# Order of the first transfers in a delta-rule attention and mixture-of-experts kernel, and matmuls of constants at its beginning

## What is computed

```python
q = (x @ Wq).reshape(b, n, H, DK)          # H = 4, DK = 128
k = (x @ Wk).reshape(b, n, H, DK)
v = (x @ Wv).reshape(b, n, H, DV)          # DV = 32
beta = jax.nn.sigmoid(x @ Wb)
k = k * jax.lax.rsqrt(jnp.sum(k * k, axis=-1, keepdims=True) + 1e-12)
def step(S, inp):                          # scanned over the 2048 positions
    q_t, k_t, v_t, b_t = inp
    pred = jnp.einsum('bhk,bhkv->bhv', k_t, S)
    delta = (v_t - pred) * b_t[..., None]
    S = S + k_t[..., :, None] * delta[..., None, :]
    return (S, jnp.einsum('bhk,bhkv->bhv', q_t, S))
```

## Time and profile before

| | us |
|---|---|
| median of 3 runs (lowest, highest) | 524.82 (523.22, 527.61) |
| the profiled execution's own time | 524.84 |
| its span | 523.1 |
| attention phase (TensorE's first expert matmul starts at) | 319.9 |
| one chunk in the steady part, from `t128_copy` of one chunk to the next (51.13 to 68.78) | 17.65 |

### The profile page before, as it was taken

The page is one execution under the profiler, slowest core; times in us unless marked ns, Lnnn a source line. Parts: engine busy times, 40 slices in busy tenths (PEclk is TensorE's granted clock), DMA queues, the critical chain, the costliest instruction groups (busy, mean ns, idle before and its releaser), DMA issues.

```text
span 523.1 us, 19041 instructions
## 1 busy us (share of the span) xinstructions
PE 467.4 (89%) x7181; PEld 389.0 (74%) x7181; DVE 314.9 (60%) x1209; ACT 327.8 (63%) x905; POOL 292.2 (56%) x445
## 2 busy tenths in 40 slices
PE   6979999999999999999898988999999999999900
PEld 4656766777667776776665677999999999999900
DVE  4435467667686676766875764644555545555345
ACT  3545668877888778878675634555555555555463
POOL 3055517638377383682753341567777767767652
PEclk9998999999999999999997999999999999999965
DMA  3367763552335514336161113354655545553376
GB/s 96 32 113 186 217 172 58 111 90 33 71 50 85 84 26 77 51 54 99 31 174 42 34 47 93 47 112 55 119 107 77 111 56 123 95 82 32 31 151 201
DMA packets 148084, 46.10 MB, mean 88 GB/s; under 512 B 107168, under 2 KB 141600, under 8 KB 148000
## 3 DMA queue, kind: packets, MB, share of 16 engines
q1 hardware_dynamic: 132848, 29.86, 29.0%
q0 software_dynamic: 13568, 9.51, 13.1%
q10 hardware_dynamic: 1584, 5.59, 2.8%
HBM read 21.39 MB, written 23.55 MB: 86 GB/s over the span
## 4 chain that ended last, share of the span: by engine, by line
PE 69%; issue 9%; ACT 9%; DMA 7%; DVE 2%; SPq 2%; POOL 1%; ACTq 0%; DVEq 0%; POOLq 0%
PE ps L1004 17%; PE ps L1015 11%; PE ps L730 5%; PE ps L681 4%; ACT TT L1126 3%; PE ps L684 2%; PE ps L761 2%; PE ps L737 2%; PE ps L812 2%; PE ps L881 2%; PE ps L896 2%; PE ps L800 2%; PE ps L1030 2%; PE ps L870 2%; PE ps L842 2%
## 5 line engine op out<-in xcount | busy, mean ns | idle before, releaser
L1784 POOL DMA_INDIRECT x_store<-xk,row x80 | 125.7, 1571 | 65.0 <-ACT xk L1275 45.5
L1603 DVE TENSOR_TENSOR hb<-ps,hs 128x320 f32<-128x320 f32 (+1 forms) x128 | 62.5, 491 | 44.6 <-ACT hs L1267 44.0
L1744 POOL DMA_INDIRECT slots_in<-x,slot x64 | 63.5, 992 | 25.4 <-issue 16.6
L1267 ACT ACTIVATE hs<-ps 128x320 f32<-128x320 f32 (+1 forms) x128 | 55.2, 435 | 32.0 <-PE ps L1004 31.2
L1004 PE MATMUL ps<-xeTh,w13h 128*128 128x320 f32 x224 | 70.5, 315 | 1.0 <-DVE xeTl L1627 1.0
L1004 PE MATMUL ps<-xeTh,w13l 128*128 128x320 f32 x224 | 69.2, 309 | 0.0
L1004 PE MATMUL ps<-xeTl,w13h 128*128 128x320 f32 x224 | 69.1, 309 | 0.0
L1015 PE MATMUL ps<-w2s,hb 128*128 128x128 f32 x512 | 64.3, 278 | 0.1
L1015 PEld LDWEIGHTS ps<-w2s,hb 128*128 128x128 f32 x512 | 59.8, 192 | 2.2 <-DVE hb L1603 0.3
L1757 POOL TENSOR_TENSOR Vk<-V,sq 128x256 f32<-128x256 f32 x16 | 10.4, 647 | 86.7 <-ACT sq L1109 86.6
L1275 ACT ACTIVATE xk<-ps,gs 128x128 f32<-128x128 f32 x80 | 24.2, 364 | 44.9 <-PE ps L1030 35.3
(11 more groups left out here) (218 smaller groups left out, 1147.5 us busy)
## 6 DMA issues: line engine op xcount, KB each, us to landing
slots_in<-zeros ACTq DMA_DIRECT2D x10, 520.0 KB, 4.2
xe<-slots_in SPq DMA_DIRECT2D x15, 325.0 KB, 2.9
w<-w_in SPq DMA_DIRECT2D x8, 448.0 KB, 4.3
xTs<-xT SPq DMA_DIRECT2D x4, 512.0 KB, 5.5
a_diag<-hb SPq DMA_DIRECT2D x64, 32.0 KB
inv<-xs SPq DMA_DIRECT2D x16, 128.0 KB
xi<-inv SPq DMA_DIRECT2D x16, 128.0 KB
xk<-x SPq DMA_DIRECT2D x8, 256.0 KB, 3.6
```

What stands on the lines that cost most here:

```text
L1267: af(hs[to, s % 4, :], ps[src, HB[fill_of(s) % 5], 0:HALF], ACT.Silu).then_inc(hs_ready, 1)
L1603: v.tensor_tensor(hb[to, par, c, HALF * g:HALF * g + HALF], ps[rows_, at, 0:HALF], hs[rows_, s % 4, :], ALU.mult).then_inc(h_ready, 1)
L1744: g.indirect_dma_start(out=xs_d[:, :], out_offset=bass.IndirectOffsetOnAxis(ap=to, axis=0), in_=x1[:, p % 2, j, k, :], in_offset=None,).th ...
L1784: g.indirect_dma_start(out=x1_d[:, :], in_=ye[:, par, i, :], in_offset=None, out_offset=bass.IndirectOffsetOnAxis(ap=row[:, par, i:i + 1], ...
```

## The change

Five edits, with the loop of SP, ACT's `clear` and the start of TensorE touched:

1. The first inverse is stored one step earlier in SP's program (step 2, after chunk 1's `load_blocks`, before chunk 2's `send_blocks`), and loaded in step 3 before chunk 2's `load_blocks` instead of behind them.
2. The second x^T chunk is issued in step 1, behind chunk 1's `send_blocks`, instead of in step 3.
3. The zeros are issued at a fixed table of places: three in ACT's steps 4 and 5, eight from (6, 2) to (7, 5).
4. `avg` is the first thing DVE sets, with a semaphore of its own, and TensorE multiplies it by itself 5 times before anything else (`begin_on(5)`).
5. `keep_on(22)` in step 4 becomes `keep_on(10)`.

```diff
--- before.py
+++ after.py
@@ -51,6 +51,8 @@
 LAST = 9
 
 YR, AR, VR = 4, 4, 4
+
+CLEARS = ((4, 3), (4, 5), (5, 1), (6, 2), (6, 3), (6, 4), (6, 5), (7, 0), (7, 2), (7, 4), (7, 5))
 
 
 def order_of_fills():
@@ -342,6 +344,7 @@
         xs_zero = sem("xs_zero")
         consts_pool = sem("consts_pool")
         consts_dve = sem("consts_dve")
+        avg_made = sem("avg_made")
         setup_mm = sem("setup_mm")
         setup_act = sem("setup_act")
         setup_dve = sem("setup_dve")
@@ -572,19 +575,24 @@
 
             for p in range(NP + LAST):
                 if p == 3:
+                    load_inverse(0)
+                at(load_blocks, p - 1)
+                if p == 2:
                     send_inverse(0)
-                at(load_blocks, p - 1)
                 if p == 4:
                     send_inverse(1)
                 if p > 4:
                     at_group(send_inverse, p - 2)
-                at(load_inverse, p - 3)
+                if p > 3:
+                    at(load_inverse, p - 3)
                 at(store_x1, p - 6)
-                if p in (3, 5, 8):
-                    load_xT(1 + (3, 5, 8).index(p))
+                if p in (5, 8):
+                    load_xT(2 + (5, 8).index(p))
                 if p in (4, 7, 11, 15):
                     load_xk((4, 7, 11, 15).index(p))
                 at(send_blocks, p)
+                if p == 1:
+                    load_xT(1)
                 if p == NP + 1:
                     load_weights(0, 0)
                     load_weights(1, 1)
@@ -918,6 +926,13 @@
                 for _ in range(n):
                     mm(ps[:, CB, 0:P], ident[:], ident[:], start=True, stop=True)
 
+            def begin_on(n):
+
+                pe.wait_ge(avg_made, 1)
+                for _ in range(n):
+                    mm(ps[:, CB, 0:P], avg[:], avg[:], start=True, stop=True)
+
+            begin_on(5)
             setup_keys()
             pe.wait_ge(wv_ld, 16)
             pe.wait_ge(setup_act, 1)
@@ -942,7 +957,7 @@
                 if p == NP + 5:
                     keep_on(36)
                 if p == 4:
-                    keep_on(22)
+                    keep_on(10)
                 at(z_32, p - 4)
                 at(outputs, p - 5)
                 at(project_x, p - 5)
@@ -1182,11 +1197,13 @@
 
             def clear(p, i):
 
-                k = 6 * (p - 6) + i - 2
-                if 0 <= k < XS_ZEROS:
+                if (p, i) not in CLEARS:
+                    return
+                k = CLEARS.index((p, i))
+                if k < XS_ZEROS:
                     act.dma_start(xs_d[k * 8 * P:(k + 1) * 8 * P, :].rearrange("(p r) d -> p (r d)", p=P),
                                   zeros[:]).then_inc(xs_zero, 16)
-                if k == XS_ZEROS:
+                else:
                     act.dma_start(xs_d[ROWS:ROWS + SPARE, :].rearrange("(p r) d -> p (r d)", p=P),
                                   zeros[:, 0:SPARE // P * W]).then_inc(xs_zero, 16)
 
@@ -1322,12 +1339,12 @@
             link = Link(dve, link_dve)
             v = nc.vector
 
+            v.memset(avg[:], 1.0 / P).then_inc(avg_made, 1)
             for t in (TT, xi, Zs, x64):
                 v.memset(t[:], 0.0)
             v.memset(eps[:], EPS)
             v.memset(tiny[:], 1e-12)
             v.memset(one[:], 1.0)
-            v.memset(avg[:], 1.0 / P)
             dve.wait_ge(consts_pool, 5)
 
             link(v.tensor_scalar(pbit[:], pidx[:], 16, None, ALU.bitwise_and))
```

## The result

| | median of the runs, us | profiled execution, us | its span, us |
|---|---|---|---|
| before, on the same chip | 525.07 (4 runs) | | |
| changed | 532.47 (531.79 to 534.68, 4 runs) | 534.68 | 532.9 |

The ratio is 1.0139, with a 95% interval of 1.0102 to 1.0177: slower by 1.4%, 7.4 us. The forecast was 523.0 us in a range that ended at 526.2. The profiled execution is the slowest of the four, so its differences from before (10 us by the span) are a little larger than those of the medians.

A forecast was written before the change was run, and what follows sets the result against it. TensorE, busy 89% of 523.1 us, was taken as the bound, with early waits on SP's queue and landings targeted. Only 1.8 us was to pass DVE's gate: 524.84 - 1.8 = 523.0 us, range 519.8 to 526.2.

The forecast's parts named there:

- keep_on(10) at nothing: Step 4 wait on TensorE: shorter fill, 2.3 instead of 5.07 us, costs at most the present low clock, so nothing.
- The beginning: TensorE's start: earlier matmuls raise the clock sooner, 1.3 us gained, bounds 1.76 gained to 0.1 lost.
- Chunk 1's blocks: SP's queue, early x^T and zeros: blocks land in 3.5 us, bounds 2.39 to 4.5; `ab` goes at 24.4.
- The inverse: SP's queue: chunk 2's `a_diag` at 28.8 instead of 27.71, `xi` at 31.1 instead of 34.19, `z_32(0)` at 35.7.
- the 3 us: Reordering on SP's queue: first inverse's load `xi` issued at 31.1 instead of 34.19.
- The gate: DVE's `scale_blocks(2)` before `z_128(0)` needs chunk 3's `ab`: L1429 at 44.5 instead of 46.30, passing 1.8 us.
- Carried to the end: Behind 55 us each step hangs on the one before, so the 1.8 us gain lasts to the end.
- a later stage reacts, which I exclude: Sign of being wrong: the gain at 50 us is gone or grown at 310 us.
- The slower one: Rival: SP's queue delays chunk 2's blocks, chunk 3's `ab` lands at 48.7; 2.4 us lost, 527.2; chance 0.07.
- a rival of its own: TensorE's wait before `z_128(0)` drops the clock to half for 1.6 us: 524.6; chance 0.18.

## Why the prediction was wrong

**keep_on(10) at nothing: the largest term that failed.** It costs 1.0%, over 5 us of the 7.4. The step was "it costs at most the low clock of now, in a stretch where TensorE is ahead of DVE by 3 us or more: nothing". I looked for its cover in the wait that it fills. In the two profiles that differ in it alone, 0.7 us lie ahead of the first milestone and 5.7 in the turn, 240 us later: there the changed kernel has 4.2 us of issue waits and a stretch at half clock, the other 0.6 us and none. That TensorE's instruction blocks are the link is likely from the cut groups, and not proven.

**The beginning: a gain, but not shown to be mine.** Predicted 1.3 us. Alone it brings 3.1 us (525.0 to 521.94), and in the profiles nearly all of it lies in the turn, so the sum's 1.3 us in the first 50 us are not borne out, and that the kernel is faster is luck by this working. I also took the 3.75 us of the first eight for the lower level of the clock; the windows view has the granted clock at 1.00 from 6 to 11 us in both profiles, so what makes them slow is open. In the changed kernel's profile the first eight took 3.53 us, and SP's first `a_diag` of interest started 0.25 us later than before.

**Chunk 1's blocks: the step that failed in the first 60 us.** "x^T behind it takes about 1.3 us of SP's queue, hidden by the landing." I priced landings alone, and those nearly right: 3.34 us where I took 3.5. (My bounds of 2.39 and 4.5 were counted from different points, the last store's issue and its end; from its end it is 1.96 us before and 2.90 changed.) Not priced was that the issue of some DMAs on SP's queue grows while the engines are full: `a_diag` +0.7 us, which zeros alone do as well, `ab` +2.3, which x^T alone does as well, the norms' load +0.9. With the start's 1.3 missing and 0.6 more for the norms' landing, chunk 2's `a_diag` goes at 32.52 instead of 28.8. I had weighed that zeros on one queue slow stores on another (4.5 us against 2.39), but read it as a price of landings only.

**The inverse: right, where x^T is not ahead of it.** SP's rows in the kernel with x^T as before lie within 0.5 us of my times, `z_32(0)` 1.3 us ahead of mine. In the changed kernel all of it is 3.3 us later and the 3 us are gone.

**The gate: half seen.** I named `ab` of chunk 3 as DVE's gate, with 1.8 us of slack. It has another beside it, in rows that I had before me. In the kernel before:

```profile
46.30 0.18 DVE L1429 SCALAR_TENSOR_TENSOR cden<-ab,denp 128x16 f32<-128x16 f32 x1
46.52 0.25 DVE L1435 RECIPROCAL c2b<-cden 128x16 f32<-128x16 f32 x1
```

`scale_blocks(2)` overwrites `xs`, so it waits for the landing of the second inverse's store; that store went at 43.45 and the load behind it, which waits for the same landing, at 46.31. The reciprocal started 0.2 us later. So the slack at this place was 0.2 us, not 1.8, and even with every transfer as I had it the gain would have been nearly nothing. I had followed the second inverse to its load and TensorE's `z_32(1)`, and not to the buffer that its store frees. In the changed kernel GpSimd's solve of it ended 2.6 us later, as it needs `ab` of chunk 1, and its store stood behind chunk 3's loads: 52.77.

**"Carried to the end" and "a later stage reacts, which I exclude": wrong** for the same reason: the turn lasts from 210.8 to 218.5 us over these kernels, whose code there is the same.

**The rivals.** The slower one had the mechanism: chunk 1's norms late, chunk 2's `a_diag` at 32.4 (measured 32.52), chunk 3's at 41.6 (40.87), its `ab` landing at 48.7 (before 49.69). It missed the second inverse (3 us more), the clock, which a rival of its own had at 1.6 us and which cost 3 in the profile, and all that `keep_on(10)` does in the turn; and I gave it 7%. The two belonged together here: the wait of 5.87 us ahead of `z_128(0)` also took the clock.

## What to carry to other kernels

When a transfer is moved forward, price it three times: on its own queue, in the issue and landing of each small DMA beside it, and for the buffers that those free. For every instruction that is called a gate, list all of its waits, also the one for a store to have left the buffer that it writes; the slack is that of the latest. And where a program of thousands of instructions meets a burst of large transfers, adding or removing a few instructions far ahead of it can go with a larger change than what they do themselves (here 2 to 6 us in the turn), so compare a control of the same length before a small gain or loss is put down to an edit.

## What the runs showed of the hardware that was not expected

- Issuing one and the same load (`ab` of chunk 1) took 0.60 us in the kernel before and 2.89 in the changed one, with x^T and zeros in flight (2.31 to 4.29 in the five others with both), 2.28 with x^T alone, 2.43 with x^T on another queue, and 0.61 with the zeros alone.
- TensorE stands still for up to 2.3 us at a time behind 262 us with nothing to wait for; the profile calls it issue. Groups of matmuls are cut in two without a dependency, in three profiles of one program length at the same place of the program. That instructions are what is missing is argued, not shown. It happens with the DMA engines 80 to 100% busy, and also with them standing still (0.01, at 303 us). The longest such wait is 0.6 to 2.1 us in the profiles with 14 matmul records fewer than before. With as many as before it is 2.3 us in the profile of the kernel before and none in the four others; with 10 or 16 more it is at most 0.9, and with 34 more 1.4.
- Behind the first wait of 1.72 us the granted clock was 0.50 (1.2 GHz) from 284 to 288 us, as it was behind the wait of 5.87 us up to 60 us; behind the second, of 1.73 us, and behind one of 1.45 us (24 matmuls in the wait) it stayed at 1.00.
- One fall of the clock for 6 to 7 us near 280 us, 3.4 us of full clock, is in all nine of the profiles with a program of the old length or shorter and in none of the nine with a longer one.
